# Mixture-of-experts feed-forward in a macaron layer: sorted assignments in blocks of 128 slots instead of every expert for every token

## The chip, the cores and the metric

One core of one Trainium2 chip. The metric is the device time of one launch in microseconds. The kernel before took 1720.37 us, median of 3 runs (1719.84 to 1720.81).

## What is computed

Two batches of 512 tokens, so 1024 tokens of width 256, all float32. The layer is x + 0.5 FFN(norm(x)), then x + attention(norm(x)), then x + 0.5 FFN(norm(x)) with the same feed-forward weights. Only the feed-forward changes:

```
scores = softmax(x @ gate_w.T)              # 16 experts
topk_w, topk_idx = top_k(scores, 4)         # 4 of 16 for each token, weights scaled to sum 1
g = x @ w_gate[e]; u = x @ w_up[e]          # width 176 for each expert e
y = sum over experts: (silu(g) * u * combine) @ w_down[e]
y = y + (silu(x @ sw_gate) * (x @ sw_up)) @ sw_down     # shared expert of width 352
```

`combine` is zero for the 12 experts that a token did not choose. There are 1024 x 4 = 4096 assignments of a token to an expert.

## The kernel before

The program is written engine by engine; each engine's list of instructions is in order, and semaphores join them. The order is: layernorm (`layernorm_*`), feed-forward 0 (`ffn_te`, `ffn_se`, `ffn_ve`), attention over 16 heads, feed-forward 1. All DMAs go through the one queue of SP (`sync`).

Layernorm works by quarters of 256 tokens: statistics on DVE (L545 to L550), the power -1/2 on POOL (L687), the scaled rows `xn` on DVE (L555), transposes on PE (L369), copies to `xT` on ACT (L468).

The feed-forward joins all hidden columns of all experts into one row of 25 chunks of 128: 3 of the shared expert (`SHARED`), 22 of the 16 experts (16 x 176 = 22 x 128). `STEPS` has 50 steps, one for each chunk and each half of 512 tokens. `up` (L392 to L405) makes gate and up products of a step, 2 x 2 matmuls with 512 moving columns; ACT takes silu (L477), DVE multiplies (L619); for the 44 steps of experts `weigh` (L621 to L625) multiplies by rows of combine weights, which SP broadcasts from DRAM (`ffn_rows`, L348). `down` (L414 to L430) adds the product with the down weights, 4 pairs of 128 tokens by 256 columns, into four PSUM banks that stay open for the whole feed-forward; matmuls with zeros open them (L420). PE runs `up(s)` and then `down(s - 2)`, so ACT and DVE have two steps to follow.

The router (`scores`, `softmax`, `compare`, `choose`, `combine`, L574 to L611) runs on DVE under the first steps; its result is transposed in step TURN (L411) and goes through DRAM (`ct_scr`). When the first half of tokens is done, `sum_rows` (L627 to L630) adds its banks to x and its next layernorm runs under the second half. The weights (9.8 MB) come in four pieces (`ffn_loads`) at the start of each feed-forward, while other data of the attention no longer needs the buffers `front` and `back`. A float32 matmul stands as two records of the matmul engine in the trace, a transpose as one.

## Time and profile before

| | us |
|---|---|
| median of 3 runs | 1720.37 |
| lowest, highest | 1719.84, 1720.81 |
| span of the profiled execution | 1722.7 |
| feed-forward 0, first matmul L403 to the attention's first matmul L919 | 15.6 to 290.6 |
| feed-forward 1, first matmul L403 to the end | 1451.1 to 1722.7 |

The profile gives of its execution the span from first to last instruction; a time of its own around that span is not given, so the span stands for it. Busy time is the time in which an engine has an instruction in work. The chain of waits follows the end of the program back through what released each instruction. Idle time of an engine that is not on that chain costs nothing.

### The profile page before, as it was taken

What the parts mean: (1) busy time and instruction counts of PE and PEld (TensorE: products, weight loads), DVE (VectorE), ACT (ScalarE), POOL (GpSimd) and SP (SyncE); (2) the same over time, 40 slices, a digit from 0 to 9 for tenths busy, and PEclk for the clock granted to TensorE, in tenths of its full rate; (3) what the DMA queues carried; (4) which work ended last, traced back from release to release, by engine and by line L of the source; (5) the groups of instructions that cost most, each with busy time, mean ns of one, the idle gap of its engine ahead of it and who ended that gap; (6) DMA issues with size and microseconds to landing.
All of it is one profiled execution on the core that took longest, in us unless ns stands there. A gap on an engine that the chain in (4) does not pass through costs nothing.

```text
span 1722.7 us, 26951 instructions
## 1 busy us (share of the span) xinstructions
PE 1572.6 (91%) x9328; PEld 1151.8 (67%) x9328; DVE 1007.9 (59%) x1663; ACT 785.1 (46%) x2409; POOL 502.2 (29%) x802
## 2 busy tenths in 40 slices
PE   7999998777998999999999899899787899999999
PEld 4565564365777777787777777777666776555555
DVE  4222232766888888889889888878656213322222
ACT  2111111756567667667767757766744221111110
POOL 1000000034535635544544553552554200000000
PEclk9999999888999999999999999999899898999999
DMA  7211111001112201201201211120123135111111
GB/s 273 57 49 54 51 49 55 21 14 39 30 38 52 63 17 52 65 27 42 61 29 29 76 37 46 39 53 27 42 69 112 43 134 229 39 49 55 50 49 55
DMA packets 131926, 102.11 MB, mean 59 GB/s; under 512 B 58224, under 2 KB 112304, under 8 KB 130512
## 3 DMA queue, kind: packets, MB, share of 16 engines
q1 hardware_dynamic: 131792, 100.39, 19.2%
q8 instruction: 76, 1.25, 0.3%
q14 instruction: 58, 0.48, 0.1%
HBM read 79.78 MB, written 20.59 MB: 58 GB/s over the span
## 4 chain that ended last, share of the span: by engine, by line
PE 72%; DVE 9%; POOL 5%; issue 5%; ACT 4%; DMA 4%; SPq 0%; DVEq 0%; POOLq 0%; ACTq 0%
PE proj L403 11%; PE proj L929 8%; PE chain L428 5%; PE tree L428 5%; PE tree L1053 5%; PE low L1053 5%; PE gates L403 5%; PE low L403 5%; DVE front L2498 4%; PE proj L975 2%; PE tree L1122 2%; POOL prodw L3232 2%; PE chain L1139 2%; PE tree L1097 2%; PE proj L1185 2%
## 5 line engine op out<-in xcount | busy, mean ns | idle before, releaser
L2498 DVE SCALAR_TENSOR_TENSOR front<-proj,pall,front 128x1022 f32<-128x1022 f32 x129 | 164.4, 1275 | 15.9 <-ACT front L1779 9.8
L3218 POOL TENSOR_TENSOR front<-front 128x512 f32<-128x512 f32 (+6 forms) x112 | 60.0, 536 | 385.8 <-PE low L1053 137.7
L929 PE MATMUL proj<-xT,wqkv 128*128 128x512 f32 x344 | 159.4, 607 | 6.8 <-DVE front L2498 6.1
L2654 DVE TENSOR_TENSOR KQ<-KQ,front 128x1024 f32<-128x1024 f32 x112 | 149.4, 1334 | 17.8 <-PE low L1053 12.2
L619 DVE TENSOR_TENSOR front<-proj,front 128x512 f32<-128x512 f32 (+1 forms) x52 | 35.9, 691 | 200.0 <-issue 162.2
L3220 POOL TENSOR_TENSOR front<-front 128x512 f32<-128x512 f32 x112 | 145.0, 1295 | 0.0
L1053 PE MATMUL tree<-KQ,front 128*128 128x128 f32 x896 | 127.3, 287 | 9.9 <-issue 7.3
L1053 PE MATMUL low<-KQ,front 128*128 128x128 f32 x896 | 124.5, 282 | 10.2 <-POOL front L3220 4.7
L477 ACT ACTIVATE front<-proj 128x512 f32<-128x512 f32 (+1 forms) x52 | 31.0, 597 | 221.6 <-PE proj L403 221.5
L619 DVE TENSOR_TENSOR front<-low,front 128x512 f32<-128x512 f32 (+1 forms) x48 | 33.2, 691 | 165.2 <-issue 149.8
L477 ACT ACTIVATE front<-gates 128x512 f32<-128x512 f32 (+1 forms) x48 | 28.6, 597 | 214.1 <-PE gates L403 214.1
L1053 PEld LDWEIGHTS tree<-KQ,front 128*128 128x128 f32 x896 | 115.2, 199 | 16.2 <-issue 13.4
L1053 PEld LDWEIGHTS low<-KQ,front 128*128 128x128 f32 x896 | 111.3, 194 | 16.0 <-issue 12.4
L929 PEld LDWEIGHTS proj<-xT,wqkv 128*128 128x128 f32 x344 | 63.3, 194 | 73.7 <-issue 63.6
L403 PE MATMUL proj<-xT,back 128*128 128x512 f32 (+1 forms) x240 | 112.3, 612 | 0.0
L3232 POOL TENSOR_TENSOR prodw<-D,W 64x15 f32<-64x15 f32 (+7 forms) x240 | 87.7, 366 | 18.8
L3235 POOL TENSOR_TENSOR W<-W,prodw 64x15 f32<-64x15 f32 (+7 forms) x240 | 76.4, 318 | 18.8
L975 PE MATMUL proj<-ident,front 128*128 128x128 f32 x384 | 57.8, 300 | 24.5 <-ACT front L1851 10.0
L403 PE MATMUL proj<-xT,front 128*128 128x512 f32 x176 | 79.1, 592 | 0.0
L403 PEld LDWEIGHTS proj<-xT,back 128*128 128x128 f32 (+1 forms) x240 | 46.4, 196 | 47.2 <-issue 45.9
L975 PEld LDWEIGHTS proj<-ident,front 128*128 128x128 f32 x384 | 48.0, 156 | 31.4 <-issue 20.7
L3245 POOL TENSOR_TENSOR ot<-ot,of 128x1024 f32<-128x1024 f32 x16 | 30.4, 1898 | 130.6 <-DVE of L2734 130.6
(255 smaller groups left out, 3666.9 us busy)
## 6 DMA issues: line engine op xcount, KB each, us to landing
front<-ct_scr SPq DMA_DIRECT2D x32, 256.0 KB, 3.4
m_img<-back SPq DMA_DIRECT2D x16, 512.0 KB, 3.2
inv<-t_img SPq DMA_DIRECT2D x16, 512.0 KB, 4.1
back<-t_img SPq DMA_DIRECT2D x16, 512.0 KB, 5.0
o_scr<-obuf SPq DMA_DIRECT2D x15, 512.0 KB, 3.8
wqkv<-in_wqkv SPq DMA_DIRECT2D x16, 384.0 KB, 3.8
front<-in_w_gu SPq DMA_DIRECT2D x2, 2816.0 KB, 16.8
front<-o_scr SPq DMA_DIRECT2D x11, 512.0 KB, 7.2
```

The source lines that it names most:

```text
L403: t = te.matmul(bank[pair_of(s) + j][0:w, :], gu_of(c)[:, k, j, 0:w], xT[:, k, b * WIDE:(b + 1) * WIDE], start=(k == 0), stop=(k == KB - 1))
L428: m = te.matmul(bank[4 + n // 2][:, n % 2 * H:(n % 2 + 1) * H], hr[0:w, s % 4, j * P:(j + 1) * P], wd_of(c)[0:w, :], start=False, stop=(c ...
L619: ve.tensor_tensor(hr[0:w, s % 4, :], bank[pair_of(s) + 1][0:w, :], sg[0:w, s % 2, :], ALU.mult).then_inc(f_act, 1)
L929: m = te.matmul(place(h, j)[:, b, :], wqkv[:, h % 2, j, k, :], xT[:, k, b * T:(b + 1) * T], start=(k == 0), stop=(k == KB - 1))
L975: m = te.transpose(FF[:, c // NC, c % NC * P:(c % NC + 1) * P], v[:, c * P:(c + 1) * P], ident[:, :])
L1053: m = te.matmul(dst, suf[:, c * P:(c + 1) * P], right, start=True, stop=True)
L2498: ve.scalar_tensor_tensor(conv[:, :, d:T], place(h, j)[:, :, 0:T - d], pall[:, h, 4 * j + 3 - d:4 * j + 4 - d], conv[:, :, d:T], ALU.mult, ...
L2654: ve.tensor_tensor(kr, kr, dl, ALU.mult).then_inc(mkq.sem, 1)
L3218: ge.tensor_tensor(dec[:, to:to + M], d[:, :, 0], d[:, :, 1], ALU.mult).then_inc(mdec.sem, 1)
L3220: ge.tensor_tensor(left, left, d[:, :, 1].unsqueeze(2).to_broadcast([P, M, 1 << l]), ALU.mult)\
L3232: ge.tensor_tensor(prodw[:, 0:rows, 0:k], D[:, j, j + 1:SUB].unsqueeze(2).to_broadcast([BN * 8, rows, k]), W[:, j, 0:k].unsqueeze(1).to_br ...
L3235: ge.tensor_tensor(W[:, j + 1:SUB, 0:k], W[:, j + 1:SUB, 0:k], prodw[:, 0:rows, 0:k], ALU.subtract)\
```

## The change

The shared expert stays as it is: 6 steps (3 chunks, 2 halves), first all chunks of half 0 and then of half 1. The layernorm of all four quarters, and all router logits, now stand ahead of it.

The 44 expert steps go. Instead, the 4096 assignments are sorted by expert. DVE makes 0/1 rows of the chosen experts; PE sums them over partitions with a triangle (`ranks`); DVE adds up totals by steps of 1, 2, 4, 8 (`scan`) and gets the slot of every assignment (`slots`), where each expert starts at a multiple of 128 slots. Four pairs of one-hot arrays (`one_hot`), multiplied on POOL by token numbers, and 32 matmuls of 47 columns (`table`) turn this into a table slot to assignment; `indices` makes the gather and scatter indices, `expert_of_block` the expert of each block. The number of blocks is fixed: 4096/128 + 15 = 47, whatever the routing.

For each block: POOL gathers 128 rows of `xn` (1 KB each) from DRAM by an indirect DMA; PE transposes them (`rows_T`); two matmuls of 352 columns give gate and up (`block_up`), at a weight address that PE holds in a register (`offsets` loads 24 and then 23 of them); ACT takes silu of 176 columns, DVE multiplies; PE transposes back (`act_T`), DVE copies; two matmuls of 256 columns (`block_down`), DVE copies to `ob`, POOL scatters 128 rows to `y_scr` in DRAM by an indirect DMA. In the end SP reads all 4096 rows back, 4.2 MB in 8 DMAs (`rows_in`), and DVE adds them with their weights in 32 instructions of 256 columns (`expert_sum`). Spare slots compute row 0 and write to spare rows.

`xn` is written to DRAM first (`rows_out`, 4 DMAs on SP) and the expert weights (10 MB) are loaded behind these. In feed-forward 1 `expert_loads(0, 14)` waits for the output projection, behind `rows_out` in SP's order. The attention's code stays the same.

```diff
-CHUNKS, SHARED = 25, 3
+SHARED = 3
 WIDE = 4 * P
+INNER = INTER // 2
+EXPERT = KB * 2 * INTER + 2 * H
+BLOCKS = TOPK * TOK // P + E - 1
+RANKS = TOPK * TB
+PAD = 4
...
-        ct_scr = nc.dram_tensor("ct_scr", (E, TOK), F32, kind="Internal").ap()
+        xn_scr = [nc.dram_tensor(f"xn_scr{f}", (TOK, H), F32, kind="Internal").ap() for f in range(2)]
+        y_scr = [nc.dram_tensor(f"y_scr{f}", (TOPK * TOK + BLOCKS * P, H), F32, kind="Internal").ap() for f in range(2)]
...
-        PARTS = ((0, SHARED), (SHARED, 14), (14, CHUNKS))
-        STEPS = [(c, b) for lo, hi in PARTS for b in range(B) for c in range(lo, hi)]
-        NS, ROUTED = len(STEPS), len(STEPS) - SHARED * B
-        TURN = 7
-        LOADS = ((0, 3), (3, 7), (7, 14), (14, CHUNKS))
-        half_done = [max(s for s, (c, b) in enumerate(STEPS) if b == k) + 1 for k in range(B)]
+        STEPS = [(c, b) for b in range(B) for c in range(SHARED)]
+        NS = len(STEPS)
...
+            shared_loads(sy)
+            rows_out(sy, 0)
+            expert_loads(sy, 0, E)
...
+            rows_in(sy, 0)
             attention_sy(sy)
             sy.wait_ge(*fin[0].of(NH - 1))
             sy.wait_ge(*fin[1].of(NH - 1))
-            for r in range(3):
-                ffn_loads(sy, r)
-            sy.wait_ge(wo_mm, TB // 2)
-            for r in range(3, len(LOADS)):
-                ffn_loads(sy, r)
-            ffn_rows(sy, 1)
+            shared_loads(sy)
+            expert_loads(sy, 14, E)
+            rows_out(sy, 1)
+            expert_loads(sy, 0, 14)
+            rows_in(sy, 1)
             for q in range(4):
                 sy.wait_ge(x_up, 8 + q + 1)
                 sy.dma_start(out[2 * q * P:2 * (q + 1) * P].rearrange("(n p) d -> p n d", p=P),
...
-        def ffn_rows(sy, f):
-            if f:
-                sy.wait_ge(f_cm, ROUTED)
-            sy.wait_ge(ct_sb, 2 * (f + 1))
-            sy.dma_start(ct_scr, combT).then_inc(s_scr, 16)
-            sy.wait_ge(s_scr, 16 * (2 * f + 1))
-            for s in range(SHARED * B, NS):
-                c, b = STEPS[s]
-                k = s - SHARED * B
-                if k >= 4:
-                    sy.wait_ge(f_cm, f * ROUTED + k - 3)
-                for e, lo, hi in experts_of(c):
-                    sy.dma_start(ct[lo:hi, k % 4, :], ct_scr[e:e + 1, b * WIDE:(b + 1) * WIDE].to_broadcast([hi - lo, WIDE]))\
-                        .then_inc(s_cb[k % 4], 16)
...
+        def expert_loads(sy, lo, hi):
+            if lo == 0 and hi < E:
+                sy.wait_ge(wo_mm, TB // 2)
+            mid = (lo + hi + 1) // 2
+            for first, last in ((lo, mid), (mid, hi)):
+                sy.dma_start(wex[:, first * EXPERT:last * EXPERT], a["w_ex"][:, first * EXPERT:last * EXPERT]).then_inc(s_we, 16)
+
+        def rows_out(sy, f):
+            for q in range(4):
+                sy.wait_ge(ln_rows, (8 * f + q + 1) * 2)
+                sy.dma_start(xn_scr[f][2 * q * P:2 * (q + 1) * P].rearrange("(n p) d -> p n d", p=P), xn[:, 2 * q:2 * q + 2, :])\
+                    .then_inc(s_xn, 16)
+
+        def rows_in(sy, f):
+            sy.wait_ge(*b_dn.of(f, BLOCKS))
+            for r in range(4):
+                sy.wait_ge(s_sc[r], 16 * (scattered(f, BLOCKS - 1, r)))
+            ranks = y_scr[f][0:TOPK * TOK].rearrange("(k n p) d -> p k n d", k=TOPK, p=P)
+            for n in range(TB):
+                sy.dma_start(y4[:, n, :, :], ranks[:, :, n, :]).then_inc(s_x[n // 2], 16)
+
+        def scattered(f, j, r):
+
+            each = [(BLOCKS - 1 - i) // 4 + 1 for i in range(4)]
+            return f * each[r] + (0 if j < r else (j - r) // 4 + 1)
...
+            def offsets(lo, hi):
+                _, values = nc.values_load_multi_w_load_instructions(
+                    eoff[0:1, lo:hi], engines=[mybir.EngineType.PE], min_val=0, max_val=(E - 1) * EXPERT,
+                    skip_runtime_bounds_check_because="clamped to the last expert where it is computed")
+                return list(values)
+
+            def rows_T(j):
+                te.wait_ge(s_g[j % 4], 16 * scattered(f, j, j % 4))
+                if j < 2:
+                    te.wait_ge(*rk_idx.of(f, 2))
+                else:
+                    te.wait_ge(*b_xc.of(f, j - 1))
+                for k in range(KB):
+                    t = te.transpose(bank[j % 2][:, k * P:(k + 1) * P], xg[:, j % 4, k * P:(k + 1) * P], ident[:, :])
+                t.then_inc(b_xt.sem, 1)
+
+            def block_up(j, at):
+                te.wait_ge(*b_xc.of(f, j + 1))
+                if j < 2:
+                    te.wait_ge(*sh_act.of(f, NS))
+                    te.wait_ge(s_we, 32 + 64 * f)
+                else:
+                    te.wait_ge(*b_act.of(f, j - 1))
+                for k in range(KB):
+                    t = te.matmul(bank[2 + j % 2][:, 0:2 * INTER], xgT[:, j % 2, k, :],
+                                  big[:, bass.ds(at + k * 2 * INTER, 2 * INTER)], start=(k == 0), stop=(k == KB - 1))
+                t.then_inc(b_up.sem, 1)
+
+            def act_T(j):
+                te.wait_ge(*b_act.of(f, j + 1))
+                if j < 2:
+                    te.wait_ge(*sh_sum.of(f, j + 1))
+                else:
+                    te.wait_ge(*b_ac.of(f, j - 1))
+                for i in range(2):
+                    t = te.transpose(bank[4 + j % 2][0:INNER, i * P:(i + 1) * P], act[:, j % 2, i * INNER:(i + 1) * INNER],
+                                     ident[:, :])
+                t.then_inc(b_at.sem, 1)
+
+            def block_down(j, at):
+                te.wait_ge(*b_ac.of(f, j + 1))
+                if j < 2:
+                    te.wait_ge(*sh_sum.of(f, j + 3))
+                else:
+                    te.wait_ge(*b_out.of(f, j - 1))
+                for i in range(2):
+                    t = te.matmul(bank[6 + j % 2][:, 0:H], aT[0:INNER, j % 2, i, :],
+                                  big[0:INNER, bass.ds(at + KB * 2 * INTER + i * H, H)], start=(i == 0), stop=(i == 1))
+                t.then_inc(b_dn.sem, 1)
...
+            for q in range(4):
+                layernorm_te(te, 2 * f, q)
+            for q in range(4):
+                logits_of(q)
+            up(0)
+            up(1)
+            up(2)
+            down(0)
+            up(3)
+            ranks()
+            down(1)
+            up(4)
+            down(2)
+            table()
+            up(5)
+            down(3)
+            te.wait_ge(*rk_eo.of(f, 1))
+            at = offsets(0, 24)
+            down(4)
+            rows_T(0)
+            rows_T(1)
+            down(5)
+            for i in range(BLOCKS + 2):
+                if i == 20:
+                    at += offsets(24, BLOCKS)
+                if i < BLOCKS:
+                    block_up(i, at[i])
+                if 1 <= i <= BLOCKS:
+                    act_T(i - 1)
+                if i >= 2:
+                    block_down(i - 2, at[i - 2])
+                if i + 2 < BLOCKS:
+                    rows_T(i + 2)
             if f == 0:
-                layernorm_te(te, 1, 2)
-                layernorm_te(te, 1, 3)
+                for q in range(4):
...
+            def one_hot(k):
+                ve.wait_ge(router, done + 27)
+                ve.tensor_tensor(hotB[:, k * TB:(k + 1) * TB, :], iota[:, 0:BLOCKS].unsqueeze(1).to_broadcast([P, TB, BLOCKS]),
+                                 place4[:, 2, k * TB:(k + 1) * TB].unsqueeze(2).to_broadcast([P, TB, BLOCKS]), ALU.is_equal)\
+                    .then_inc(rk_a.sem, 1)
+                ve.tensor_tensor(hotA[k], iota.unsqueeze(1).to_broadcast([P, TB, P]),
+                                 place4[:, 3, k * TB:(k + 1) * TB].unsqueeze(2).to_broadcast([P, TB, P]), ALU.is_equal)\
+                    .then_inc(rk_a.sem, 1)
...
+            def block_act(j):
+                ve.wait_ge(*b_sl.of(f, j + 1))
+                if j >= 2:
+                    ve.wait_ge(*b_at.of(f, j - 1))
+                ve.tensor_tensor(act[:, j % 2, :], sil[:, j % 2, :], bank[2 + j % 2][:, INTER:2 * INTER], ALU.mult)\
+                    .then_inc(b_act.sem, 1)
+
+            def act_copy(j):
+                ve.wait_ge(*b_at.of(f, j + 1))
+                if j >= 2:
+                    ve.wait_ge(*b_dn.of(f, j - 1))
+                ve.tensor_copy(aT[0:INNER, j % 2, :, :].rearrange("p i t -> p (i t)"), bank[4 + j % 2][0:INNER, 0:2 * P])\
+                    .then_inc(b_ac.sem, 1)
+
+            def out_copy(j):
+                ve.wait_ge(*b_dn.of(f, j + 1))
+                if j >= 4:
+                    ve.wait_ge(s_sc[j % 4], 16 * scattered(f, j - 4, j % 4))
+                ve.tensor_copy(ob[:, j % 4, :], bank[6 + j % 2][:, 0:H]).then_inc(b_out.sem, 1)
+
+            def expert_sum(q):
+                ve.wait_ge(s_x[q], 16 + 32 * (f + 1))
+                ve.wait_ge(router, done + ROUTER)
+                ve.wait_ge(*sh_sum.of(f, 4))
+                at = q * 6
+                for k in range(TOPK):
+                    for i in range(2):
+                        n = 2 * q + i
+                        if k:
+                            ve.wait_ge(*y_sum.of(f, at + 2 * (k - 1) + i + 1))
+                        m = ve.scalar_tensor_tensor(x[:, n, :], y4[:, n, k, :], wk[:, k * TB + n:k * TB + n + 1], x[:, n, :],
+                                                    ALU.mult, ALU.add)
+                        if k < TOPK - 1:
+                            m.then_inc(y_sum.sem, 1)
+                m.then_inc(x_up, 1)
...
+            for q in range(4):
+            softmax()
+            act_of(0)
+            compare(0, E // 2)
+            compare(E // 2, E)
+            choose()
+            counts()
+            scan()
+            slots()
+            one_hot(0)
+            one_hot(1)
+            one_hot(2)
+            one_hot(3)
+            expert_of_block()
+            sum_rows(0)
+            sum_rows(1)
+            indices()
+            weights_of()
+            sum_rows(3)
+            for i in range(BLOCKS + 2):
+                if i < BLOCKS:
+                    block_act(i)
+                if 1 <= i <= BLOCKS:
+                    act_copy(i - 1)
+                if i >= 2:
+                    out_copy(i - 2)
+            for q in range(4):
+                expert_sum(q)
+                if f == 0:
+                    layernorm_rows(ve, 1, q)
+                    if q:
+                        layernorm_out(ve, 1, q - 1)
...
+        def ffn_ge(ge, f):
+            def gather(j):
+                if j >= 4:
+                    ge.wait_ge(*b_xt.of(f, j - 3))
+                ge.indirect_dma_start(out=xg[:, j % 4, :], out_offset=None, in_=xn_scr[f],
+                                      in_offset=bass.IndirectOffsetOnAxis(ap=gidx[:, j:j + 1], axis=0))\
+                    .then_inc(s_g[j % 4], 16)
+
+            def scatter(j):
+                ge.wait_ge(*b_out.of(f, j + 1))
+                ge.indirect_dma_start(out=y_scr[f], out_offset=bass.IndirectOffsetOnAxis(ap=sidx[:, j:j + 1], axis=0),
+                                      in_=ob[:, j % 4, :], in_offset=None).then_inc(s_sc[j % 4], 16)
+
+            for k in range(TOPK):
+                piece = hotB[:, k * TB:(k + 1) * TB, :]
+                ge.wait_ge(*rk_a.of(f, 2 * k + 1))
+                ge.tensor_tensor(piece, piece, value[:, k * TB:(k + 1) * TB].unsqueeze(2).to_broadcast([P, TB, BLOCKS]), ALU.mult)\
+                    .then_inc(rk_b.sem, 1)
+            ge.wait_ge(s_xn, 64 * (f + 1))
+            ge.wait_ge(*rk_idx.of(f, 1))
+            for j in range(4):
+                gather(j)
+            ge.wait_ge(*rk_idx.of(f, 2))
+            for j in range(BLOCKS):
+                if j + 4 < BLOCKS:
+                    gather(j + 4)
+                scatter(j)
```

## Rows read from the trace of the kernel before

**Rows 1.** The page, part 1: busy time of each engine and its share of the span.

```profile
PE 1572.6 (91%) x9328; PEld 1151.8 (67%) x9328; DVE 1007.9 (59%) x1663; ACT 785.1 (46%) x2409; POOL 502.2 (29%) x802
```

**Rows 2.** Busy time by stretch: us, PE, PEld, DVE, ACT, POOL, clock, DMA share, GB/s.

```profile
50.50:277.00 226.50, 226.50 (x713) 133.57 (x712) 59.74 (x101) 28.40 (x48) 4.89 (x3) 1.00 0.20 60
...
1487.00:1719.00 232.00, 231.67 (x730) 137.29 (x728) 58.28 (x91) 27.32 (x46) 0.00 (x0) 1.00 0.17 53
```

**Rows 3.** Chain of waits, first feed-forward: start us, us, what.

```profile
11.98 3.60 PE tree L378 x16
...
15.58 5.24 PE proj L403 x8
20.82 0.88 PE chain L369 x8
...
30.32 1.72 PE tree L420 x4
...
50.96 3.43 PE proj L403 x8
54.40 1.73 PE chain L428 x8
```

**Rows 4.** The same chain, end of the first feed-forward.

```profile
278.03 5.20 PE chain L428 x24
...
288.77 1.11 PE chain L369 x4
...
290.60 6.05 PE proj L919 x8
```

**Rows 5.** Instructions in time, second feed-forward: start us, us, engine, line.

```profile
1449.62 0.73 DVE L555 TENSOR_SCALAR KQ<-x,mv,rstd 128x256 f32<-128x256 f32 x2 [0.26 <-POOL rstd L687]
...
1718.71 1.29 DVE L630 SCALAR_TENSOR_TENSOR x<-chain,x 128x512 f32<-128x512 f32 x2 [3.23 <-PE chain L428]
```

**Rows 6.** Groups of instructions on DVE: last figures before the bar: busy us, mean ns.

```profile
L2654 DVE TENSOR_TENSOR KQ<-KQ,front 128x1024 f32<-128x1024 f32 x112 | 149.4, 1334 | 17.8 <-PE low L1053 12.2 <-PE tree L1053 5.6
...
L619 DVE TENSOR_TENSOR front<-proj,front 128x512 f32<-128x512 f32 x50 | 34.6, 692 | 200.0 <-issue 162.2 <-PE proj L403 37.8
...
L2712 DVE COPY St<-chain 128x128 f32<-128x128 f32 x32 | 9.0, 285 | 26.8 <-PE chain L1172 26.8
```

**Rows 7.** DVE in time, the router of the first feed-forward.

```profile
28.21 0.28 DVE L582 TENSOR_REDUCE rowv<-score 128x8 f32<-128x128 f32 x1
...
28.76 0.29 DVE L586 TENSOR_TENSOR score<-score,rowv 128x128 f32<-128x128 f32 x1
```

**Rows 8.** The SP queue in time: one DMA issue.

```profile
58.11 0.33 SPq L340 DMA_DIRECT2D ct_scr<-front  x1
```

**Rows 9.** Groups on POOL.

```profile
L3245 POOL TENSOR_TENSOR ot<-ot,of 128x1024 f32<-128x1024 f32 x16 | 30.4, 1898 | 130.6 <-DVE of L2734 130.6
...
L3218 POOL TENSOR_TENSOR front<-front 128x512 f32<-128x512 f32 x16 | 16.7, 1042 | 138.6 <-PE tree L1062 127.4 <-PE low L1062 11.2
```

**Rows 10.** DMA issues: count, KB each, median us from issue to landing.

```profile
back<-t_img SPq DMA_DIRECT2D x16, 512.0 KB, 5.0
...
front<-ct_scr SPq DMA_DIRECT2D x16, 128.0 KB, 2.9
...
x<-in_x SPq DMA_DIRECT2D x4, 256.0 KB, 3.7
...
out<-x SPq DMA_DIRECT2D x4, 256.0 KB, 2.8
```

**Rows 11.** Busy time of short stretches, columns as in the second group.

```profile
16.00:20.00 4.00, 4.00 (x7) 1.58 (x6) 0.00 (x0) 0.60 (x1) 0.00 (x0) 1.00 1.02 429
...
308.00:312.00 4.00, 1.91 (x5) 0.95 (x6) 3.93 (x4) 2.09 (x2) 0.00 (x0) 1.00 0.31 98
324.00:328.00 4.00, 1.65 (x12) 1.44 (x11) 3.96 (x4) 3.68 (x25) 0.00 (x0) 0.76 0.00 2
1448.00:1452.00 4.00, 4.00 (x18) 3.57 (x17) 2.32 (x10) 1.87 (x2) 0.78 (x1) 0.50 0.99 422
```

440 lines of the change are left out of this document (274 added, 166 removed).

## The prediction

> **What bounds the kernel now.** I read the page first: PE is busy 91% of the span [rows 1]. The busy time by stretch then asks whether that holds in the part that changes: from 50.5 to 277 us and from 1487 to 1719 us, the expert steps of the two feed-forwards, PE has no idle time at 1.00 of the clock (2.4 GHz), while DVE has 26%, ACT 13% and the DMA engines 20% [rows 2]. The chain of waits agrees: in the feed-forward it runs over PE alone, 3.43 us for the four matmuls of `up` (8 records of 0.43 us, 512 columns) and 1.73 us for `down` (8 records of 0.216 us, 256 columns) [rows 3]. So a step costs 5.16 us, and 44 expert steps cost 227 us, twice. Whatever takes columns away from PE shortens the chain, until something else is late.
>
> **What goes.** 2 x 227 us of PE. The broadcasts of combine weights and `weigh` go too; they lay beside PE and give nothing.
>
> **What a block costs PE.** By the same rows: two matmuls of 352 columns, 4 records of 0.43 x 352/512 = 0.295, 1.18 us; two of 256 columns, 4 x 0.216 = 0.86 us; four transposes at 0.88/8 = 0.11, 0.44 us [rows 3]. Together 2.49 us, and 47 blocks cost 117 us. Were PE the bound, each feed-forward would lose 110 us. The loads of block addresses into registers have no row; I count 2 us for the first, and nothing for the second and for address arithmetic, which the sequencer does while the array works; at most some 0.3 us a block.
>
> **The chain that takes PE's place.** POOL's order is gather(4), scatter(0), gather(5), scatter(1) and so on. scatter(j) waits for `out_copy(j)`, thus for `block_down(j)`, which PE runs in turn j + 2. Behind it on POOL's queue stands gather(j + 5), and PE wants its rows in turn j + 3, directly behind `block_down(j + 1)`. That leaves one turn for: copy and signal, descriptors of the scatter (S), descriptors of the gather (G), landing of the rows (L). Call this C. With PE's work W = 2.49 us, d(j) the end of `block_down(j)`, the rows of block m can be transposed at max(d(m-4), d(m-5) + C), and d(m-3) follows W later. Where C is over a turn, two turns take C + W, so a turn is P = (C + W)/2. POOL alone would ask for S + G, PE alone for W; P is the largest. DVE, with a product and two copies, 0.35 + 0.42 + 0.42, and ACT stay under P.
>
> Copy: 285 ns for 128 columns [rows 6], plus 0.13 for 128 more, plus signals, 0.6 us. S and G: no indirect DMA is in the trace. The nearest row below is one issue on SP, 0.33 us [rows 8]; above, the longest two-input pass of POOL over 128 partitions in the page, 1.90 us [rows 9]. 128 addresses taken one by one by POOL should be clearly more than a fixed pattern; I take the middle, 1.1 us. L: a 128 KB load lands 2.9 us after its issue starts, a strided 512 KB one 5.0 us [rows 10]; less the issue itself that is 2.45 us, with ends of 1.9 and 4.6. So C = 0.6 + 1.1 + 1.1 + 2.45 = 5.25 and P = 3.87 us. The ends: C = 3.2, P = 2.85; C = 9.0, P = 5.7. Spread over 47 blocks the old expert steps cost 227/47 = 4.83 us, so the loop gains 0.96 us a block where it could have gained 2.34.
>
> The Trainium skill, "DMA: Bandwidth & Descriptors", section on the anatomy of a DMA from the GpSimd path, gives about 2.0 us plus bytes by 436 GB/s for setup and completion of one such DMA. By that G + L would be an estimated 2.3 us in place of 3.55, C 4.0, P 3.25 and the time 1647 us; no row here shows such a DMA, and it is a rival below.
>
> **The head.** Feed-forward 0 now puts all layernorm and all logits ahead of the shared steps. Two more tables of 128 KB hold back POOL's first instruction by some 0.9 us; the last rows are normalised at 14.2, transposed at 15.3; 32 logit records take 3.60 per 16 while the clock is at 1.2 GHz and half at 2.4 [rows 3]: I take 5.2. First `up` at 20.5 us, before at 15.58. In feed-forward 1 the rows are ready at 1450.35 [rows 5]; PE was at 0.50 of the clock there [rows 11], so with transposes and some 6 us of logits `up` starts at 1457.5, before at 1451.1.
>
> From there to the first block: `up(0)` to `up(3)` and `down(0)` with its zeros, 3.9 + 3 x 3.43 + 3.45 = 17.6; `ranks` and its copy 0.9; `act_of(3)` 0.69 [rows 6]; then DVE is the path, where formerly PE was: ten small dependent operations at 0.28 to 0.29 [rows 7], 2.9; `slots` 2.4; four times one-hot rows of 376 and 1024 elements, 0.55 + 1.33 [rows 6], 7.5. That is 32.0. POOL's products (up to 1.04 each, [rows 9]) are under it but the last. The last 16 records of `table`, at the low clock since PE stood still, 3.6, make it 35.6. Then PE: `up(5)` partly at the low clock 5.2, `down(3)` with zeros 3.45, registers 2, `down(4)`, `rows_T` and `down(5)` 1.73 + 0.44 + 1.73. Sum 50 us. `down(1)`, `up(4)` and `down(2)` lie beside DVE. The first gathers are issued some 9 us earlier and are hidden. Blocks start at 70.3 and at 1507.4. The weights, 10 MB at 429 GB/s [rows 11], 23 us and behind `rows_out` on SP, are in by 45 and 1475: nothing.
>
> **Loop and tail.** d(0) is 5.0 us after the start; 44 turns follow at P, 170.3 us; the last two without gathers, 3.5. Then copy, scatter and its landing, 0.45 + 1.1 + 2.4 = 3.95; nothing covers it. The first two reads of 512 KB, issued and landed, 5.2 (3.7 for 256 KB, [rows 10]). Then DVE: eight sums of 256 elements for each quarter, 0.42 each, 3.4; the DMAs bring a quarter (1 MB) in 2.4 to 3.4 us, just under it. In feed-forward 0 each quarter also has statistics and output of the next layernorm, 1.98, so 4 x 5.38 = 21.5; last power and output 1.5; transposes and copy 1.7. The old kernel did half of this under PE's second half. Tail 33.9, before 290.60 - 283.23 = 7.4 [rows 4]. So the attention starts at 70.3 + 5.0 + 170.3 + 3.5 + 33.9 = 283.0, formerly 290.6: 7.6 earlier. POOL's memset of `back` ends before its first power is wanted. The attention itself keeps its time; its first weights are loaded already.
>
> Feed-forward 1: 1507.4 + 5.0 + 170.3 + 3.5 + 3.95 + 5.2 + 13.5, then output issue and landing 3.3 (2.8, [rows 10]) = 1712.2, less 7.6 = 1704.6. Formerly 1722.7: the last sums began at 1718.71 [rows 5]. Change -18.1 us. The span stands 2.3 us above the median of the runs, 1720.4, so I predict 1702 us: 220 us of PE work freed, 121 of it lost to the gather chain (2 x 44 x 1.38) and some 81 to heads and tails.
>
> **Rivals.** The total moves by 88 us for each us of P, 44 for each us of C.
>
> (a) Descriptors or landings are cheap: P about 3.25, 55 us less, 1647 us; with both at their lower ends P is 2.85 and the time 1612. For it: SP's issue takes 0.33 us. Against: SP's issue writes no list of 128 addresses. 0.27.
>
> (b) Indirect DMAs are dear, slower than before: S and G at POOL's 1.90 us, C = 6.85, P = 4.67, +70, 1772 us. The place is the pair scatter(j), gather(j + 5) on POOL's queue; it decides from P = 4.08, that is S = G = 1.3 us. For it: POOL's passes of 1 to 2 us [rows 9]. Against: a descriptor list isn't a pass over data. 0.27.
>
> (c) The clock. PE is at work for 2.49 of 3.87 us. In 308 to 312 us it was busy 1.91 of 4 at clock 1.00; in 324 to 328, 1.65 of 4 at 0.76 [rows 11]. If the gaps take it to 1.2 GHz, W is 4.98, P is 5.12 and the time 1812; but then PE is nearly always busy, and with PE busy throughout it is 1.00 [rows 2], so a mean between is likelier. 0.08.
> The Trainium skill, "TensorE: Matmul & The Clock Gate", says that the throttled state is the default and activity releases it. The traces agree in both feed-forwards' starts, and by that rule a full-time fall would not last.
>
> (d) The change doesn't cut PE's work: no. Blocks are 47 by the code, and the columns are counted.
>
> (e) My own chain, P between 3.6 and 4.2, 1678 to 1731 us: 0.38; some 0.06 of it near no change and 0.06 slower. Faster: 0.27 + 0.27 = 0.54; within 0.2% (3.4 us, about what a measurement can tell from no change) 0.05; slower 0.41, that is (b), (c) and the upper edge of (e). The range takes in most of (a) and (b): 1635 to 1790.
>
> **What would show it.** Right: in the block loop PE idles about 1.4 us a turn, in front of the transposes of `rows_T`, released by the gather's DMA; pairs of turns last 7.7 us; POOL waits at the scatter for DVE's copy. Wrong: PE without gaps in the loop and turns of 2.5 us; or POOL without idle time, turns of S + G; or PE's idle time in front of `block_up` or `block_down`, which would put DVE or ACT in the chain. For the head: blocks begin 50 us after the first `up`, with DVE without idle time in the one-hot arrays. For the tail: 34 us from the last `block_down` to L919's place. The number is wrong if S, G or L are off: each us of any of them is 44 us of time.

## The result, and the profile after

The changed kernel takes 1742.5 us (median of 4 runs, 1736.0 to 1755.8), the kernel before 1720.6 in the same comparison: ratio 1.0131, interval 1.0082 to 1.018. It is slower by 22 us where 18 us less was predicted; 1742.5 lies in the range. The profiled execution is the longest of the four, 1755.8 us with a span of 1754.0. I compare it with the profiled one of before (span 1722.7): +31.3 us.

From the page of the kernel after (times in us, shares of the span):

```profile
span 1754.0 us, 28006 instructions
PE 1445.1 (82%) x9168; PEld 1108.1 (63%) x9168; DVE 1062.1 (61%) x1921; ACT 791.4 (45%) x2501; POOL 701.7 (40%) x998
PEclk9899986878999999999999999999999798898986
...
PE 57%; DVE 15%; DMA 11%; issue 6%; POOL 5%; ACT 5%; SPq 0%; DVEq 0%; POOLq 0%; ACTq 0%
...
L974 POOL DMA_INDIRECT y_scr<-big,sidx x94 | 93.1, 990 | 203.6 <-DVE big L887 197.5
L522 PE MATMUL proj<-ident,tg 128*128 128x128 f32 x188 | 41.7, 308 | 108.4 <-DMA tg<-xn_scr,gidx 108.3
L968 POOL DMA_INDIRECT tg<-xn_scr,gidx x94 | 91.6, 975 | 53.8 <-issue 25.0
```

PE's busy time fell from 91% to 82% of the span [rows 1]; that is 127 us, not the 220 us of freed work. A part of what is missing is the low clock: in the two loops PE is busy 287 us, where 94 blocks at 2.49 us are 234. In the chain of waits DMAs rose from 4% to 11% of the span; the gathers of `xn_scr` are 8% of the span. PE stood 108 us in front of the transposes of gathered rows. POOL stood 197 us in front of its scatters.

The busy time by stretch: first `up` to first block, block loop and tail of feed-forward 0, then the same three of feed-forward 1. Columns as in [rows 2].

```profile
22.00:77.60 55.60, 54.06 (x178) 35.21 (x179) 33.87 (x94) 5.82 (x10) 14.70 (x10) 0.85 0.51 193
77.60:276.00 198.40, 142.76 (x562) 95.31 (x560) 52.44 (x143) 31.65 (x92) 85.85 (x89) 0.91 0.19 58
276.00:307.00 31.00, 4.34 (x16) 2.86 (x16) 20.30 (x61) 2.10 (x4) 8.40 (x7) 0.52 0.45 147
1474.00:1528.00 54.00, 52.19 (x180) 33.45 (x181) 33.86 (x94) 5.82 (x10) 11.81 (x9) 0.83 0.32 131
1528.00:1729.50 201.50, 144.23 (x561) 95.79 (x559) 52.19 (x143) 31.65 (x92) 85.57 (x88) 0.90 0.20 57
1729.50:1754.00 24.50, 0.00 (x0) 0.00 (x0) 13.17 (x33) 0.00 (x0) 1.82 (x2) 0.54 0.71 230
```

The attention starts at 307.4 us instead of 290.6. From there to the first `up` of feed-forward 1 it is 1167.0 us, where 1166.9 were predicted (1160.5 before, when fewer logits stood in front of `up`). So the difference to the prediction is settled in the feed-forwards. That stretch scatters by itself: in the profiles of this kernel and of its variants below it takes 1151.6 to 1169.8 us, though nothing in it was changed. The loops are therefore compared on their own as well as the times. The loops take 198 and 201.5 us where 178.8 were predicted, and the heads 55.5 and 53.6 where 50 were.

**The predicted chain is there.** This is the chain of waits of the kernel after, cut to 140 to 148 us of the loop:

```profile
139.85 0.44 DVE big L887
140.29 0.27 issue
140.56 0.99 POOL y_scr L974
141.55 0.30 issue
141.85 2.78 DMA tg<-xn_scr,gidx
```

Copy, descriptors of the scatter, 0.30 between the two, descriptors of the gather with their landing, and then the transposes at 144.67 us. Line L522 is `rows_T`, L887 `out_copy`, L974 the scatter and L968 the gather. From the timeline of the same turns:

```profile
140.43 0.44 PE L522 MATMUL proj<-ident,tg 128*128 128x128 f32 x2 [0.61 <-DMA tg<-xn_scr,gidx]
143.20 0.42 DVE L887 COPY big<-chain 128x256 f32<-128x256 f32 x1
143.90 0.99 POOL L974 DMA_INDIRECT y_scr<-big,sidx  x1 [1.08 <-DVE big L887]
144.67 0.44 PE L522 MATMUL proj<-ident,tg 128*128 128x128 f32 x2 [1.51 <-DMA tg<-xn_scr,gidx]
145.20 0.97 POOL L968 DMA_INDIRECT tg<-xn_scr,gidx  x1 [0.30 <-PE proj L522]
147.98 0.44 PE L522 MATMUL proj<-ident,tg 128*128 128x128 f32 x2 [0.58 <-DMA tg<-xn_scr,gidx]
```

Two turns take 147.98 - 140.43 = 7.55 us, 3.78 a turn (3.87 predicted). But the mean from the 5th turn to the last is 4.37 us in feed-forward 0 and 4.45 in feed-forward 1. Three things show in the longer turns.

**Late rows.** Here are two blocks from the timeline later in the loop. The gather at 177.24 fetches a block of which the routing of these inputs fills one slot; 127 spare slots all read row 0. The one at 234.71 fetches a block that is all spare.

```profile
177.24 0.97 POOL L968 DMA_INDIRECT tg<-xn_scr,gidx  x1 [0.31 <-issue]
181.07 0.44 PE L522 MATMUL proj<-ident,tg 128*128 128x128 f32 x2 [1.98 <-DMA tg<-xn_scr,gidx]
...
234.71 0.97 POOL L968 DMA_INDIRECT tg<-xn_scr,gidx  x1 [0.30 <-issue]
238.66 0.44 PE L522 MATMUL proj<-ident,tg 128*128 128x128 f32 x2 [3.25 <-DMA tg<-xn_scr,gidx]
```

From the end of descriptors to the transposes it is 2.86 and 2.98 us, where the full block above had 144.67 - 142.82 = 1.85. So the DMA itself takes about a microsecond longer. In feed-forward 0, 39 of the 47 blocks hold assignments, and 15 of the 47 have more than half their slots spare, 8 of these all.

**The clock.** Two stretches of four us behind each other:

```profile
178.00:182.00 4.00, 2.02 (x11) 1.32 (x9) 1.09 (x3) 0.69 (x2) 2.07 (x3) 0.98 0.25 68
182.00:186.00 4.00, 4.00 (x13) 2.75 (x12) 1.09 (x3) 0.57 (x2) 0.11 (x1) 0.59 0.11 33
```

After PE's wait of 1.98 us the granted clock falls to near its lower level (1.2 GHz) and the turn that follows, which waits for nothing, takes 4.26 us (181.07 to 185.33) instead of 2.5 to 2.7. Not every such wait does this: behind 2.31 us of waiting for block 5 of this loop the next turn took 2.57 us, behind 2.21 us for block 7 it took 4.03.

**The address registers.** Once in each loop PE loads 23 block addresses. From the timeline:

```profile
152.74 0.44 PE L522 MATMUL proj<-ident,tg 128*128 128x128 f32 x2 [2.02 <-DMA tg<-xn_scr,gidx]
155.25 2.71 PE L533 MATMUL gates<-big 128*128 x4 [2.07 <-issue]
159.88 0.64 PE L522 MATMUL proj<-ident,tg 128*128 128x128 f32 x2
```

The turn takes 7.14 us: 2.07 of idle time at the load, just behind 2.02 for the gather, and the clock falls to 0.50 with it. How long PE stands at this load depends on the rest: 1.9 to 2.2 us in the kernels that keep the changed kernel's order of gather and scatter, 0.30 and 0.18 in sp_scatter below, where PE never waits for rows.

### The profile page after: what moved, and what is told of

Same layout as the page of the kernel before. It is cut to its first block, busy times and chain, and to the rows that moved or that the text cites. A ratio compares the mean times of both kernels' runs of the same rounds, so it can differ in the third digit from the quotient of the medians.

```text
span 1754.0 us, 28006 instructions
## 1 busy us (share of the span) xinstructions
PE 1445.1 (82%) x9168; PEld 1108.1 (63%) x9168; DVE 1062.1 (61%) x1921; ACT 791.4 (45%) x2501; POOL 701.7 (40%) x998
## 4 chain that ended last, share of the span: by engine, by line
PE 57%; DVE 15%; DMA 11%; issue 6%; POOL 5%; ACT 5%; SPq 0%; DVEq 0%; POOLq 0%; ACTq 0%
PE proj L1235 8%; DMA tg<-xn_scr,gidx 8%; PE low L1359 5%; DVE big L2804 5%; PE tree L1359 5%; PE chain L555 3%; POOL y_scr L974 3%; PE low L533 2%; PE gates L533 2%; PE chain L1445 2%; PE proj L1281 2%; PE tree L1428 2%; PE tree L1403 2%; PE proj L1491 2%; PE proj L1275 1%
## 5 line engine op out<-in xcount | busy, mean ns | idle before, releaser
L974 POOL DMA_INDIRECT y_scr<-big,sidx x94 | 93.1, 990 | 203.6 <-DVE big L887 197.5
L2804 DVE SCALAR_TENSOR_TENSOR big<-proj,pall,big 128x1022 f32<-128x1022 f32 x129 | 164.4, 1275 | 15.6 <-ACT big L2085 9.5
L2960 DVE TENSOR_TENSOR KQ<-KQ,big 128x1024 f32<-128x1024 f32 x112 | 151.5, 1352 | 17.8 <-PE low L1359 12.1
L3526 POOL TENSOR_TENSOR big<-big 128x512 f32<-128x512 f32 x112 | 143.3, 1280 | 0.0
L1359 PE MATMUL tree<-KQ,big 128*128 128x128 f32 x896 | 126.7, 286 | 11.4 <-issue 8.7
L1359 PE MATMUL low<-KQ,big 128*128 128x128 f32 x896 | 125.8, 284 | 10.6 <-POOL big L3526 4.7
L522 PE MATMUL proj<-ident,tg 128*128 128x128 f32 x188 | 41.7, 308 | 108.4 <-DMA tg<-xn_scr,gidx 108.3
L1359 PEld LDWEIGHTS tree<-KQ,big 128*128 128x128 f32 x896 | 114.5, 198 | 17.8 <-issue 14.8
L1359 PEld LDWEIGHTS low<-KQ,big 128*128 128x128 f32 x896 | 112.4, 195 | 16.6 <-issue 12.5
L968 POOL DMA_INDIRECT tg<-xn_scr,gidx x94 | 91.6, 975 | 53.8 <-issue 25.0
L555 PE MATMUL chain<-big 88*128 x376 | 111.5, 425 | 0.0
L522 PEld LDWEIGHTS proj<-ident,tg 128*128 128x128 f32 x188 | 23.4, 152 | 138.9 <-DMA tg<-xn_scr,gidx 133.7
```

The lines of the kernel that those rows point to most:

```text
L522: t = te.transpose(bank[j % 2][:, k * P:(k + 1) * P], xg[:, j % 4, k * P:(k + 1) * P], ident[:, :])
L555: t = te.matmul(bank[6 + j % 2][:, 0:H], aT[0:INNER, j % 2, i, :], big[0:INNER, bass.ds(at + KB * 2 * INTER + i * H, H)], start=(i == 0), ...
L968: ge.indirect_dma_start(out=xg[:, j % 4, :], out_offset=None, in_=xn_scr[f], in_offset=bass.IndirectOffsetOnAxis(ap=gidx[:, j:j + 1], axis ...
L974: ge.indirect_dma_start(out=y_scr[f], out_offset=bass.IndirectOffsetOnAxis(ap=sidx[:, j:j + 1], axis=0), in_=ob[:, j % 4, :], in_offset=No ...
L1359: m = te.matmul(dst, suf[:, c * P:(c + 1) * P], right, start=True, stop=True)
L2804: ve.scalar_tensor_tensor(conv[:, :, d:T], place(h, j)[:, :, 0:T - d], pall[:, h, 4 * j + 3 - d:4 * j + 4 - d], conv[:, :, d:T], ALU.mult, ...
```

## The experiments

Theory A: the order on POOL's queue, scatter(j) ahead of gather(j + 5), sets the turn; late rows and falls of the clock come on top. Rivals: the indirect DMAs themselves are dear (POOL or the landing bounds whatever the order), or PE is slow in the loop for a reason of its own.

### The order of gather and scatter

lag2 (lag1 is the same with 1 in place of 2):

```diff
-            for j in range(BLOCKS):
+            for j in range(BLOCKS + 2):
                 if j + 4 < BLOCKS:
                     gather(j + 4)
-                scatter(j)
+                if j >= 2:
+                    scatter(j - 2)
```

> POOL issues gather(j + 4) and then scatter(j - 2) in place of scatter(j); nothing else changes. Theory A, the chain through POOL's queue (scatter waits for the block's output, the next gather stands behind it, PE waits for its rows): the chain is cut, a turn falls from 4.37 and 4.45 us to what POOL needs for one gather and one scatter with their handovers, 0.97 + 0.99 + 2 x 0.30 = 2.56 us; 2 x 41 turns x 1.8 = 148 us less than the changed kernel's 1742, so about 1595 us, PE without idle time in front of the transposes, clock 1.00 in the loop. Theory B, the rows land late for themselves (DMA latency, the scatters' writes in the way): turns stay over 4 us, time within 15 us of 1742. Theory C, the loop is held by PE's addresses in registers: turns fall little, PE idles elsewhere.

Measured 1590.9 us (1587.7 to 1593.2), ratio 0.9235 to the kernel before (0.9206 to 0.9263). The loops take 119.2 and 120.3 us. Two turns of the timeline of lag2:

```profile
104.59 0.38 PE L522 MATMUL proj<-ident,tg 128*128 128x128 f32 x2
104.99 0.97 POOL L968 DMA_INDIRECT tg<-xn_scr,gidx  x1 [0.30 <-PE proj L522]
106.27 0.99 POOL L974 DMA_INDIRECT y_scr<-big,sidx  x1 [0.30 <-issue]
107.08 0.38 PE L522 MATMUL proj<-ident,tg 128*128 128x128 f32 x2
107.56 0.97 POOL L968 DMA_INDIRECT tg<-xn_scr,gidx  x1 [0.30 <-PE proj L522]
```

and its loop in the busy time by stretch:

```profile
77.00:197.00 120.00, 117.60 (x561) 85.81 (x559) 52.66 (x143) 31.66 (x92) 86.30 (x88) 1.00 0.33 97
```

Most turns are 2.49 us, just the W that was predicted for PE alone (the means, with the load of registers, are 2.55 and 2.57); PE is busy 98% at clock 1.00, with the same gathers, scatters and spare rows. Theory A holds: 150 us hang on the order of two instructions, on this chip.

> POOL issues gather(j + 4) and then scatter(j - 1). Theory A: gather(j + 5) now waits for block j - 1, one turn earlier, so three turns take the chain and PE's work: (4.7 + 2.5 x 2)/3 is 3.2 us at most, by the same counting where one more turn is left; with POOL's own 2.56 a turn is between 2.6 and 3.2 us, the time 1595 to 1645 us. Theory B: over 1720 us.

1609.3 us in a single run, turns of 2.82. One turn of lag is nearly enough.

sp_scatter leaves the scatter by indices out. SP writes the blocks' outputs in slot order instead, so the rows that are read back aren't the tokens':

```diff
-            sy.wait_ge(*b_dn.of(f, BLOCKS))
+            for j in range(BLOCKS):
+                sy.wait_ge(*b_out.of(f, j + 1))
+                sy.dma_start(y_scr[f][j * P:(j + 1) * P], ob[:, j % 4, :]).then_inc(s_sc[j % 4], 16)
...
-                scatter(j)
```

> The scatter by indices is left out: SP writes each block of 128 output rows to DRAM in slot order (so the rows that are read back aren't those of the tokens), POOL only gathers. Theory A: no scatter is in front of a gather, POOL needs 1.27 us a turn, and the turn is PE's own work, 2.5 to 2.6 us; 1590 us. Against lag2 it tells what POOL's descriptor work still costs there: nothing or under 0.1 us a turn. Theory B (landings late by themselves): turns over 4 us.

1585.6 us in a single run, only 5 under lag2; the loops are 117.5 and 117.3 us against 119.2 and 120.3. So POOL's 0.99 us for a scatter costs 2 to 3 us a loop once no gather waits for DVE behind it. It isn't free, though: in lag2 POOL goes from gather to gather in 107.56 - 104.99 = 2.57 us, and PE needs 2.49. So the gather starts 5.3 us ahead of the transposes for block 7 and only 4.1 us ahead for block 21. That lead suffices for most of the 47 blocks; by my estimate from these turns a longer loop would go at POOL's 2.57.

### Clock and late rows

fill2 gives PE work in front of its wait, two matmuls that nobody reads:

```diff
                 if i + 2 < BLOCKS:
+                    for _ in range(2):
+                        te.matmul(bank[i % 2][:, 256:512], ident[:, :], xT[:, 0, 0:256], start=True, stop=True)
                     rows_T(i + 2)
```

> Two extra matmuls of 256 columns (0.86 us of PE, result unused) in each turn ahead of the transposes, where PE waits for rows anyway; POOL's order is that of the changed kernel. Theory A, clock: the turns are longer than the 3.78 us of the chain because PE falls to 1.2 GHz after waits of 2.3 us and more; with work in the wait it stays at 2.4 GHz, mean clock of the loop from 0.90 to 0.98 or more, turns 3.8 us, about 45 us faster than 1742, so some 1695 us, though PE does 81 us more work. Rival, late landings of their own: clock may rise, turns stay at 4.3 to 4.5 us or grow by the filling, 1742 or up to 1780 us.

1727.2 us (1720.9 to 1733.5): 15 less than the changed kernel, not the 47 expected. The clock in the loops is 0.99, and the turns are still 4.09 and 4.16: about half of what they had over 3.78 was clock. That the 0.86 us of filling cost nothing themselves isn't shown.

spread lets a spare slot gather the row of its partition number instead of row 0:

```diff
-                ve.tensor_scalar(gidx[:, 0:BLOCKS], which[:, 3, 0:BLOCKS], -1.0, 0.0, ALU.add, ALU.max).then_inc(rk_idx.sem, 1)
+                ve.tensor_scalar(which[:, 5, 0:BLOCKS], got, 0.0, value[:, 0:1], ALU.is_equal, ALU.mult).then_inc(router, 1)
...
+                ve.scalar_tensor_tensor(gidx[:, 0:BLOCKS], which[:, 3, 0:BLOCKS], -1.0, which[:, 5, 0:BLOCKS], ALU.add, ALU.add)\
+                    .then_inc(rk_idx.sem, 1)
```

> The changed kernel, but a spare slot gathers the row with the number of its partition instead of row 0 (one small DVE operation more in each feed-forward); POOL's order is the changed kernel's. In the changed kernel's trace the software DMA packets of full blocks end 1.35 to 1.5 us after the gather's descriptors are written, those of blocks with 89 or more spare slots 2.0 to 2.8 us. Theory D, many reads of one DRAM row are served one after the other: all gathers now end at 1.4 to 1.5 us, turns lose 0.2 to 0.3 us (16 of 47 blocks, 1.0 us each, half of it because two turns share a chain), 20 to 35 us faster than 1742, more if fewer waits then let PE's clock fall. Rival E, the late packets come from traffic of the scatters or from how blocks lie in time: unchanged, within 8 us.

1724.2 us (1713.2 to 1734.3). Where PE waits for a gather, the time from the end of its descriptors to the transposes falls to 1.93 and 1.84 us in the mean, from 2.15 in the changed kernel. The eight blocks that are all spare show it best: in feed-forward 0 it is 2.65 to 2.99 us in fill2 and 1.79 to 1.90 with spread reads on the same chip (spread_again below; the eighth is 3.33, where PE itself came late). The turns are 4.18 and 4.12, at a clock of 0.91 and 0.93.

> Both: spare slots read different rows, and two extra matmuls of 256 columns (0.86 us) fill PE's wait ahead of the transposes. If late rows (D) and the clock (A) are together what the turns have over the chain of 3.78 us, turns are now 3.8 us at a clock of 0.99 or more, about 45 us less than 1742 in all and 20 to 25 less than fill2's 1727: 1695 to 1705. If a third cause is left, turns stay at 4.0 or more and the time over 1715.

Both: 1713.3 us (1705.6 to 1718.9), ratio 0.9942 (0.9914 to 0.997), turns of 3.86 and 3.99. The load of registers is 3.4 us of a loop, 0.08 a turn; with it the chain's 3.78 gives the 3.86 of the first loop, and 0.13 of the second stay open. That the first meets the predicted 3.87 is luck, since the prediction had a longer chain and no load. What stays above 1702 is mostly the heads. Each edit alone gives 15 to 18 us and both 29. The loops alone say the same: the two loops of a profile sum to 399.5 us in the changed kernel, 377.3 in fill2, 375.1 in spread and 360.8 in spread_fill2 (357.6 were predicted). spread and spread_fill2 ran on another chip (15) than fill2 (1).

### The same edits on lag2, and a miss

> lag2 with spare slots that read different rows. With gathers issued some two turns ahead, a row that lands 1 us late is covered, so both theories D and E expect no difference to lag2's 1591 us (within 4 us; one small operation more in each head).

1626.0 us (1617.2 to 1633.1), 35 above lag2 where no difference was expected, with loops of 138.9 and 139.6 us.

lag2_dve is lag2 with the products of the one-hot arrays on DVE instead of POOL (L980), for the head:

```diff
+                piece = hotB[:, k * TB:(k + 1) * TB, :]
+                ve.wait_ge(*rk_a.of(f, 2 * k + 1))
+                ve.tensor_tensor(piece, piece, value[:, k * TB:(k + 1) * TB].unsqueeze(2).to_broadcast([P, TB, BLOCKS]), ALU.mult)\
+                    .then_inc(rk_b.sem, 1)
...
-            for k in range(TOPK):
```

> lag2 with the products of the one-hot rows and token numbers (4 of 376 elements for each feed-forward) on DVE instead of POOL. In the changed kernel's trace DVE's compare of 376 elements takes 0.55 us when POOL is idle and 1.16 beside POOL's product, and POOL's takes 1.73. If the two hold each other up, the compares all take 0.55 us, the products 0.5 to 0.6 us on DVE, and the last record of the table's matmuls comes 1 to 2 us earlier: 1589 us. If not, DVE's part grows by 4 x 0.55 and the time by 2 to 4 us.

1635.1 us in a single run. Every compare of 376 elements now takes 0.54 to 0.55 us and every product 0.54, so the two did hold each other up, and a pass (a pair of one-hot arrays, four in a feed-forward) takes 2.06 us instead of 2.22. But the heads are 54.9 and 52.5 us against 55.1 and 55.3 in lag2, no clear gain; the last part says why. And again a loop of 142.5 and 139.2 us. These two had run on another chip (15) than lag2 (1), so the next question was whether edit or chip did it.

> The kernel of lag2 unchanged, run beside lag2_spread on one chip, because lag2_spread and lag2_dve came in another call than lag2. Theory 'the edit': moving the spare slots' reads made the loop longer, then this is near 1591 (1586 to 1597), with loops of 119 to 120 us, and lag2_spread is some 35 us above it. Theory 'the run': the loop of 47 blocks at 2.5 us is at the mercy of something that differs between chips or calls, then the two stand within 8 us of each other, either both near 1591 or both near 1626 with loops of about 139 us.

> The kernel of lag2_spread unchanged, beside lag2_again. Theory 'the edit': 1617 to 1633 as before, some 35 us above lag2_again. Theory 'the run': within 8 us of lag2_again, on whichever side that falls.

lag2 unchanged took 1632.2 us (1620.8 to 1633.1) and lag2_spread 1624.9 beside it; before stood at 1721.0. So the theory of the edit is dead: the same program takes 1591 or 1632 us. This is the timeline of lag2_again where it loses time:

```profile
100.02 0.38 PE L522 MATMUL proj<-ident,tg 128*128 128x128 f32 x2
100.24 1.35 PE L533 MATMUL gates<-big 128*128 x4
101.43 0.38 PE L544 MATMUL tree<-ident,big 128*88 128x128 f32 x2
102.05 1.13 PE L555 MATMUL chain<-big 88*128 x4 [0.24 <-issue]
103.01 0.38 PE L522 MATMUL proj<-ident,tg 128*128 128x128 f32 x2
104.33 0.42 DVE L887 COPY big<-chain 128x256 f32<-128x256 f32 x1 [2.43 <-PE chain L555]
104.38 0.37 ACT L622 COPY big<-proj 128x256 f32<-128x256 f32 x1 [4.71 <-PE proj L522]
```

PE's transposes are on record at 100.02 us. ACT's copy of them follows 0.4 us after their start in lag2; here it starts at 104.38, 4.36 after. DVE stands still for 2.43 us until 104.33 beside it, and PE runs into both. By these records the engines behind PE start 1 to 4 us late, in bunches; I call these late signals, though the profile doesn't tell whether the signals or the recorded times of PE are off. They begin with block 7 in both loops and mostly return after three to five turns, 16 or 17 blocks of 47 in each. The granted clock is 0.98 in this loop, and packets and bytes of every DMA queue are those of lag2.

### All on one chip

Since two causes rested on runs on different chips, I ran them beside the changed kernel.

> The changed kernel itself, on one chip with the three below, because lag2 showed that a loop can take 119 us on one chip and 139 us on another. Theory 'both causes are in the kernel': near 1742 (1732 to 1756), turns of 4.37 and 4.45 us. Theory 'part of its excess is the chip's': off 1742 by more than 10 us, while the kernel before stays within 3 us of 1721.

> The two extra matmuls of a turn again, now on the chip of after_again. If the clock's falls cost the changed kernel 15 us, this is 10 to 20 us under after_again; if that difference was between chips, it is within 5 us of it.

> The spare slots' reads spread again, now on the chip of after_again. If late rows cost the changed kernel 18 us, this is 12 to 24 us under after_again; if that difference was between chips, it is within 5 us of it.

> The scatter put behind the gather of the same turn, on the chip of the three above. If a PE without pauses is what draws the late signals seen in lag2_again, this one with its small waits has fewer of them, and is nearer to 1609 than lag2 was to 1591: 1609 to 1625. If late signals come whatever PE does: 1640 to 1650. On a chip without them: 1609.

| us, one chip (1) | median | lowest, highest | turns |
|---|---|---|---|
| before | 1722.5 | 1714.0, 1728.5 | |
| changed kernel | 1740.1 | 1725.6, 1749.0 | 4.12, 4.44 |
| fill2 | 1724.7 | 1720.6, 1731.5 | 4.13, 4.09 |
| spread | 1724.2 | 1713.6, 1730.3 | 4.09, 4.18 |
| lag1 | 1615.2 | 1612.1, 1616.1 | 2.88, 2.89 |

Both differences come again: 15 and 16 us. With four runs of a kernel that scatters this much that alone is thin, but taken with the first comparisons seven of its eight runs lie above all 20 runs of fill2 (at most 1733.5) and all 20 of spread (at most 1734.3). The changed kernel scatters by 23 us from run to run, far more than lag1 with 4. Its profiled execution here was its shortest, 1725.6, with a clock of 0.95 in the first loop, where the one above had 0.91. That loop took 186.3 us, no more than fill2's in its first profile (186.7), and the two loops of the profiles here sum to 385.7 in the changed kernel, 376.4 in fill2 and 377.3 in spread: how often the clock falls differs from run to run.

> The kernel of lag2 on one chip with lag1_spread and lag1_third. On a chip with late signals of PE near 1630, on one without them near 1591.

> The kernel of lag1 again: 1609 to 1616 on any chip if its small waits keep the late signals away; if they come by the chip alone, then 1630 or more where lag2_third is at 1630.

> The scatter one turn late and the spare slots' reads spread. The waits that lag1 has left (turns of 3.3 to 3.6 us among turns of 2.5) are late rows of blocks with spare slots: without them the turn falls from 2.8 to about 2.65, 10 us less over both feed-forwards: 1600 to 1606. If a PE without pauses draws the late signals, then on a chip where lag2_third shows them this one shows some too, and is not below lag1_third.

lag2 1625.8 us (1619.4 to 1631.3), lag1 1633.1 (1632.3 to 1633.3), lag1_spread 1632.8 (1624.9 to 1644.7), before 1719.9. All three now show the late signals: in lag1 the loops are 144 us where they were 130 and 133. So the small pauses of lag1 don't keep them away; and spreading shows no gain behind them.

The chips on which the runs were made sort them. The profiles of lag2, sp_scatter and lag1 (twice) on chip 1 have no copy of ACT more than 0.7 us behind the start of PE's transposes. All seven profiles of lagged kernels on chips 6, 7 and 15 have 12 to 18 blocks of 47 in each loop in which it is over 0.8 us, up to 4.4. The kernels with the changed kernel's order, spread and spread_fill2, have none on chip 15, beside lag2_spread and lag2_dve, which do. So they came with certain chips, or with something that differed between these sessions, and there only in the loops of 2.5 to 2.9 us a turn. Only chip 1 was used in more than one comparison. What they are stays open. On every chip on which they ran, lag1 and lag2 beat the kernel before, by 5 to 8%; the changed kernel was set beside them on chip 1 alone.

## Why the prediction was wrong

- **What goes, what a block costs PE, which resource comes next**: right. W was put at 2.49 us and is 2.49 where nothing waits (lag2). PE's idle time stands in front of `rows_T`, released by the gather's DMA; POOL waits at the scatter for DVE's copy, as it was said.
- **S and G** (1.1 each, taken as the middle of 0.33 and 1.90): 0.99 and 0.975, and 0.30 between the two that I had no row for. **Copy** 0.6: 0.70 from its start to the scatter's. **L** 2.45: 1.85 for full blocks. From the copy's start to the transposes it is 147.98 - 143.20 = 4.78 us, and from the transposes to the copy's start 143.20 - 140.43 = 2.77, where W alone is 2.49. Counted as in the prediction, from 2.49 us after the transposes, C is 5.06 instead of 5.25, and (C + W)/2 = 3.78: the chain itself was a little shorter than the prediction's. That it came so near is partly luck, as L was 0.6 too long and the 0.30 and the signals were missing. The Trainium skill, "DMA: Bandwidth & Descriptors", section on the anatomy of a DMA from the GpSimd path, would by my estimate have made G + L 2.3 us; it is 2.8 to 2.9 here, between that and my 3.55.
- **The step that failed is "a turn is P = (C + W)/2"** with one C and one W for all turns. The mean is 4.37 and 4.45. Rival (c) took the clock as a case of its own at 0.08 and priced only a fall for the whole time; in fact it is a part of my own case (e): the chain makes waits, the long ones among them make the clock fall for a turn, and W is then 4.3. The Trainium skill, "TensorE: Matmul & The Clock Gate", section "HAM oscillation — how this bites in real kernels", describes a loop whose waits for DMAs let the clock fall again each time; the trace agrees in that the clock falls behind a wait (0.59 after 1.98 us), and differs in that it doesn't behind each of them; I had read it only as a bound on rival (c). The other part, late rows of spare slots, was not in the prediction at all: L was one number. Both facts were in the code, that 47 blocks are fixed and that spare slots all read row 0. Loops: +19.2 and +22.7 us against the 178.8 predicted.
- **The second load of registers**, counted at nothing: 2.07 us and a fallen clock, 3.4 us over a turn of 3.78, once a feed-forward; it is in the +19.2. The first load, counted at 2 us, has no idle time of PE in front of it in either head.
- **The head**, 50 us predicted, 55.5 and 53.6. Here the step that failed is that DVE is the path through the one-hot arrays and only the last 16 records of `table` come on top. From the timeline and the busy time by stretch of the kernel after:

```profile
49.01 0.55 DVE L802 TENSOR_TENSOR big<-rtab,place 128x376 f32<-128x376 f32 x1
49.64 1.73 POOL L980 TENSOR_TENSOR big<-big,rtab 128x376 f32<-128x376 f32 x1 [24.82 <-DVE big L802]
50.62 1.16 DVE L802 TENSOR_TENSOR big<-rtab,place 128x376 f32<-128x376 f32 x1
51.52 6.46 PE L505 MATMUL proj<-big,KQ 128*128 128x47 f32 x32 [1.54 <-POOL big L980]
57.76 3.63 PE L505 MATMUL proj<-big,ot 128*128 128x47 f32 x16
61.17 3.63 PE L505 MATMUL proj<-big,obuf 128*128 128x47 f32 x16
51.50:64.60 13.10, 13.08 (x65) 13.10 (x65) 10.22 (x12) 0.00 (x0) 5.19 (x3) 0.53 0.38 138
```

  L505 is `table`. Its 64 records run without a pause from 51.52 to 64.8 us, 13.3 us at a clock of 0.53, with the weight loads (PEld) busy for all of it. DVE and POOL hand over a pair of arrays every 2.2 us, and PE needs 3.3 to 3.6 for the 16 records of one. From the first one-hot row to the end of `table` it is 64.8 - 49.0 = 15.8 us, where 7.5 + 3.6 = 11.1 were predicted: 4.7 us more. `up` to the first one-hot row took 26.8 instead of 24.5, 2.3 us more, for which `up(0)` alone is enough (6.5 us, partly at the low clock, instead of 3.9). Behind `table`, `up(5)` took 0.5 more and the registers 2 less. In feed-forward 1 the same stretch from one-hot row to the end of `table` took 14.2 us. The price of POOL's product was bounded by 1.04 and is 1.73, and DVE's compare takes 1.16 beside it instead of 0.55, but only the first product stands in front of PE; that is why lag2_dve could not shorten the head by much. First `up` 22.2 where 20.5 was predicted: 1.7 us.
- **The tail** was 31.6 and 24.6 us against 33.9 and 26.0: right, a little dear.
- **In sum**: feed-forward 0 +24.4 us (start +1.7, head +5.7, loop +19.2, tail -2.3), feed-forward 1 +25.1 more (head +3.7, loop +22.7, tail -1.4). Together 49 over 1704.6; in the median of the runs 40 over 1702. The chances followed from that: at 88 us for each us of P, a turn 0.5 too short moves the time by 44 us and changes the sign.

## What to carry to other kernels

Before an instruction that fetches goes behind one that waits for a result on the same queue, ask for whom the second is urgent: a scatter nobody waits for stood ahead of a gather that PE was waiting for, and exchanging them with a lag of a turn or two was worth 125 to 150 us of 1742 on one chip (on three others the changed kernel wasn't run beside them). In a loop that hangs on a chain of latencies, don't price all turns alike: look for the turn in which the clock falls behind a wait, for the one that loads registers, and for blocks whose gathers all read one row. Where one engine feeds another piece by piece, price the slower of the two at the clock that it will have: here it was PE's small matmuls, not DVE. And repeat a winning kernel on a second chip before a difference of 2% is put down to an edit.

## What the runs showed of the hardware

- An indirect DMA of 128 rows of 1 KB costs POOL 0.97 us as a gather and 0.99 as a scatter, 0.30 from the one to the next, and full rows can be used 1.85 us after the descriptors; with all or nearly all of the 128 indices alike it is 2.6 to 3.0 us, and spreading them over rows brings it back (1.79 to 1.90 in seven of the eight all-spare blocks of spread_again's first loop). Gather and scatter in turn thus take POOL 2.57 us a block (lag2).
- Behind a wait of PE of 1.98 us for a gather the granted clock drops from 0.98 to 0.59 in the next stretch of 4 us; behind another of 2.31 us it doesn't; the two extra matmuls of fill2 in front of the wait keep it at 0.99 over the loops.
- 64 PE records of 47 columns, each with its own load of 128 by 128 weights, take 13.3 us at a mean clock of 0.53, and the weight loads fill all of that time (`table` in feed-forward 0).
- The same program (lag2) took 1591 us on chip 1 and 1632 and 1626 on chips 6 and 7, with the kernel before at 1723, 1721 and 1720. In the slower ones ACT and DVE start up to 4.4 us after the PE instruction they wait for, from block 7 on. In the changed kernel's two profiles, and in those of its variants fill2, spread and spread_fill2, every copy of ACT starts within 0.8 us of PE's transposes; spread and spread_fill2 ran on chip 15, where lag2_spread and lag2_dve show the late starts.
